# Cross-attention row stacks: permuted weight columns for longer reads, one write of the score rows, six filling matmuls before each first half

## The reference, cut to what matters

```
x = layernorm(x + causal_attention(x))            # one head, width 256
Q, K, V = x Wq' + bq, ctx Wk' + bk, ctx Wv' + bv  # 16 heads of 16
per head, blocks of 128 queries and keys:
  local = softmax(Q_b K_b' / 4) V_b
  cross = softmax(Q_b K_w' / 4) V_w               # w: blocks b-1, b, b+1 inside the sequence
x = layernorm(x + (local + cross) Wo' + bo)
x = layernorm(x + top2_of_8_experts(x) + shared_expert(x))
```

## Time and profile before

| | |
|---|---|
| median of 3 runs | 935.84 us (932.71 to 937.98) |
| profiled execution, its own time | 933.65 us |
| its span, first to last instruction | 931.9 us |
| mean granted TensorE clock | 0.907 of full |
| PE busy, share of the span | 89% |
| DVE, ACT, POOL busy | 43%, 37%, 26% |
| DMA traffic | 76.83 MB, mean 82 GB/s |

### The profile page before, as it was taken

One profiled execution on the slowest core, in us unless ns is written; L12 is line 12 of the kernel. 1 busy time (PEld: TensorE's weight loads), 2 busy tenths in 40 slices (PEclk: granted clock), 3 DMA queues, 4 the chain that ended last, 5 costly groups with the idle time before them and its releaser, 6 DMA issues. The chain is left out here.

```text
span 931.9 us, 15553 instructions
## 1 busy us (share of the span) xinstructions
PE 830.1 (89%) x4992; PEld 626.3 (67%) x4993; DVE 397.5 (43%) x746; ACT 346.7 (37%) x898; POOL 242.0 (26%) x258
## 2 busy tenths in 40 slices
PE   6689988999898989999579998999999999999930
PEld 4567765777567656766479997666777777666620
DVE  4736574568346844452376552211222222222216
ACT  1122454346343633255254430333333333333313
POOL 6912111123111401020416775211111111111106
PEclk9987995799669975999889999999999999999975
DMA  9962133121404080300191115541111101111035
GB/s 305 159 178 51 47 94 91 44 52 50 135 2 91 19 231 3 70 4 2 49 363 42 57 52 131 182 158 34 34 34 34 33 29 34 34 34 32 19 108 179
DMA packets 61045, 76.83 MB, mean 82 GB/s; under 512 B 16112, under 2 KB 41584, under 8 KB 60880
## 3 DMA queue, kind: packets, MB, share of 16 engines
q1 hardware_dynamic: 57600, 66.99, 25.9%
q0 software_dynamic: 3408, 9.34, 2.8%
HBM read 50.82 MB, written 24.98 MB: 81 GB/s over the span
## 5 line engine op out<-in xcount | busy, mean ns | idle before, releaser
L1023 DVE TENSOR_REDUCE mx<-ps 128x4 f32<-128x512 f32 (+1 forms) x128 | 104.4, 821 | 95.4 <-PE ps L1507 93.9
L1694 PE MATMUL ps<-we,hT 128*128 x624 | 142.8, 382 | 2.5 <-ACT hT L795 2.5
L1694 PEld LDWEIGHTS ps<-we,hT 128*128 128x128 f32 x624 | 119.7, 192 | 35.5 <-issue 20.9
L1674 PE MATMUL ps<-we,xT 128*128 x312 | 140.6, 593 | 1.9 <-issue 1.9
L1224 DVE COPY hp<-ps 128x512 f32<-128x512 f32 x78 | 50.2, 686 | 158.5 <-PE ps L1674 158.5
L1507 PE MATMUL ps<-k_stack,q_stack 96*128 96x256 f32 (+1 forms) x256 | 88.9, 441 | 16.2 <-DMA q_stack<-q_rows 14.2
L795 ACT ACTIVATE hT<-ps,b1T 128x128 f32<-128x128 f32 x312 | 84.9, 383 | 35.2 <-PE ps L1685 35.2
L1674 PEld LDWEIGHTS ps<-we,xT 128*128 128x128 f32 x312 | 56.2, 190 | 58.1 <-issue 58.1
L697 ACT ACTIVATE pT<-ps 128x256 f32<-128x256 f32 x128 | 49.2, 385 | 117.9 <-PE ps L1522 113.1
L1507 PEld LDWEIGHTS ps<-k_stack,q_stack 96*128 96x128 f32 x256 | 50.6, 246 | 54.5 <-issue 24.4
L590 ACT ACTIVATE xT<-ps 128x256 f32<-128x256 f32 x39 | 14.9, 384 | 180.9 <-PE ps L1657 180.9
(11 more groups left out here) (214 smaller groups left out, 1246.1 us busy)
## 6 DMA issues: line engine op xcount, KB each, us to landing
we<-in_w SPq DMA_DIRECT2D x16, 1024.0 KB, 10.6
k_stack<-k_rows SPq DMA_DIRECT2D x24, 256.0 KB, 4.0
q_stack<-q_rows SPq DMA_DIRECT2D x96, 64.0 KB, 4.1
slot_rows<-attn SPq DMA_DIRECT2D x1, 4992.0 KB, 25.0
xs<-slot_rows SPq DMA_DIRECT2D x39, 128.0 KB, 2.1
k_rows<-k_s SPq DMA_DIRECT2D x16, 256.0 KB, 2.3
q_rows<-q_s SPq DMA_DIRECT2D x16, 256.0 KB, 2.8
yl<-pair_out SPq DMA_DIRECT2D x4, 1024.0 KB, 9.5
```

The source lines that it names most:

```text
L1023: nc.vector.tensor_reduce(mx[:, n, 2 * p:2 * p + 2, r0:r0 + nb], ps[:, 2 * (u % 2):2 * (u % 2) + 2, 0:nb * P].rearrange("p h (b k) -> p h ...
L1674: m = nc.tensor.matmul(ps[:, 2 + c, :], xT[:, q, k, :], w[:, bass.ds(e, 1), k * HID + c * 512:k * HID + (c + 1) * 512].rearrange("p o n -> ...
L1694: m = nc.tensor.matmul(ps[:, 6, 0:D], hT[:, c, :], w[:, bass.ds(e, 1), KD * HID + c * D:KD * HID + (c + 1) * D].rearrange("p o n -> p (o n)"),
```

## The change

1. The columns of the cross-attention's `Wq` and `Wk` and their biases are permuted (on the host, where the weights are laid out), the same way for both, so that the 16 or 32 rows of a pair are interleaved: row `4 r + g` is row `r` of pair `g`. A `k_stack` read then takes, for each partition, 4 adjacent rows (8 KB), a `q_stack` read 2 adjacent rows (4 KB). Heads of `q_stack` change their place (`at` below), and so do the heads in `aug`.
2. High and low parts have semaphores of their own, and the order of the `q_stack` reads is by part first.
3. The four aug rows go in one DMA.
4. At the end of each `project2` with a `c` (three of them) PE waits for the combination (`cb_out`) and runs six `keep_clock` matmuls into bank 0.

```diff
+WARM_Q = 6
...
-                    sp.dma_start(rows[h, part], src[:, h, part, :].bitcast(F)).then_inc(away[h], 16)
+                    sp.dma_start(rows[h, part], src[:, h, part, :].bitcast(F)).then_inc(away[2 * h + part], 16)
...
-                sp.wait_ge(k_away[h], 32 * b + 32)
-                for sec, part in ((0, 0), (2, 0), (1, 1)):
-                    sp.dma_start(k_stack[32 * sec:32 * sec + 32, h * PAIRS:(h + 1) * PAIRS, :].bitcast(F),
-                                 k_rows[h, part].rearrange("(g p) t -> p g t", g=PAIRS)).then_inc(stacked[h], 16)
-                sp.wait_ge(q_away[h], 32 * b + 32)
+            def stack_keys(b, h):
+                for part, secs in ((0, (0, 2)), (1, (1,))):
+                    sp.wait_ge(k_away[2 * h + part], 16 * b + 16)
+                    for sec in secs:
+                        sp.dma_start(k_stack[32 * sec:32 * sec + 32, h * PAIRS:(h + 1) * PAIRS, :].bitcast(F),
+                                     k_rows[h, part].rearrange("(r g) t -> r g t", g=PAIRS)).then_inc(stacked[h], 16)
+            def stack_queries(b, h):
                 for part_done, g0 in ((stacked, 0), (stacked_late, PAIRS // 2)):
-                    for par in range(2):
-                        for sec, part in enumerate((0, 0, 1)):
-                            r = 32 * sec + 16 * par
-                            at = h * HALF + 2 * g0 + par
-                            sp.dma_start(q_stack[r:r + 16, at:at + HALF // 2 - 1:2, :].bitcast(F),
-                                         q_rows[h, part].rearrange("(g a p) t -> a p g t", g=PAIRS, a=2)
-                                         [par][:, g0:g0 + PAIRS // 2, :]).then_inc(part_done[h], 16)
+                    for part, secs in ((0, (0, 1)), (1, (2,))):
+                        sp.wait_ge(q_away[2 * h + part], 16 * b + 16)
+                        for sec in secs:
+                            for par in range(2):
+                                r, at = 32 * sec + 16 * par, h * HALF + PAIRS * par + g0
+                                sp.dma_start(q_stack[r:r + 16, at:at + PAIRS // 2, :].bitcast(F),
+                                             q_rows[h, part].rearrange("(a r g) t -> a r g t", a=2, g=PAIRS)
+                                             [par][:, g0:g0 + PAIRS // 2, :]).then_inc(part_done[h], 16)
...
-                for r in range(4):
-                    sp.dma_start(q_stack[96 + r:97 + r, h * HALF:(h + 1) * HALF, :].bitcast(F),
-                                 augT[r * HALF:(r + 1) * HALF, :].bitcast(F)).then_inc(s["aug_in"], 16)
+                sp.dma_start(q_stack[96:100, h * HALF:(h + 1) * HALF, :].bitcast(F),
+                             augT[:, :].bitcast(F)).then_inc(s["aug_in"], 16)
...
-                    nc.vector.tensor_copy(aug[:, :, 0, :], ncross[:, :, :]).then_inc(s["aug_step"], 1)
+                    nc.vector.tensor_copy(by_pair(aug[:, :, 0, :]), ncross4).then_inc(s["aug_step"], 1)
...
-                if c is None:
-                    keep_clock(WARM, bank=0)
+                if c is not None:
+                    pe.wait_ge(s["cb_out"], c + 1)
+                keep_clock(WARM if c is None else WARM_Q, bank=0)
                 pe.wait_ge(s["qk2_lo"], 4 * b + 4)
...
-                                                 q_stack[0:96, ha * HALF + 2 * p + j, n * P:(n + 1) * P],
+                                                 q_stack[0:96, ha * HALF + PAIRS * j + p, n * P:(n + 1) * P],
...
-                        qv = q_stack[:, 2 * p:2 * p + 2, :]
+                        at = hc * HALF + p % PAIRS
+                        qv = q_stack[:, at:at + PAIRS + 1:PAIRS, :]
...
+    order = np.arange(D).reshape(2, PAIRS, 2, DH).transpose(0, 2, 3, 1).reshape(D)
+    for n in ("L0_xattn_Wq", "L0_xattn_Wk"):
+        lay[n] = lay[n][:, order]
```

More of the change, by code:

```diff
@@ L222, in build @@
                                             for n in ("xs_in", "yw_sent", "st_step", "st_sent"))
-        k_away, q_away, stacked, stacked_late = ([sem(f"s_{n}{h}") for h in range(2)]
-                                                 for n in ("k_away", "q_away", "stacked", "stacked_late"))
+        k_away, q_away = ([sem(f"s_{n}_away{h}_{part}") for h in range(2) for part in ("hi", "lo")] for n in "kq")
+        stacked, stacked_late = ([sem(f"s_{n}{h}") for h in range(2)] for n in ("stacked", "stacked_late"))
         yl_in = [sem(f"s_yl_in{b}") for b in range(B)]
@@ L298, in body @@
                     sp.wait_ge(s["b_ps"], 2 * UNITS * (2 * b - 1))
-                stack(b, 0)
-                keys_away(b, 1)
-                queries_away(b, 1)
+                stack_keys(b, 0)
+                stack_queries(b, 0)
+                rows_away(b, 1, k_rows, k_s, k_away, 1)
+                rows_away(b, 1, q_rows, q_s, q_away, 2)
                 if not last:
@@ L314, in body @@
                     sp.wait_ge(s["b_ps"], 2 * UNITS * (2 * b))
-                stack(b, 1)
+                stack_keys(b, 1)
+                stack_queries(b, 1)
                 if not last:
@@ L319, in body @@
                         .then_inc(s["c_raw_in"], 16)
-                    keys_away(b + 1, 0)
+                    rows_away(b + 1, 0, k_rows, k_s, k_away, 1)
                 aug_rows(b, 1)
                 if not last:
-                    queries_away(b + 1, 0)
-            keys_away(0, 0)
-            queries_away(0, 0)
+                    rows_away(b + 1, 0, q_rows, q_s, q_away, 2)
+            rows_away(0, 0, k_rows, k_s, k_away, 1)
+            rows_away(0, 0, q_rows, q_s, q_away, 2)
             body(0, True, False)
@@ L596, in aug_rows @@
                 if free:
-                    act.wait_ge(s["aug_in"], 64 * a)
+                    act.wait_ge(s["aug_in"], 16 * a)
                 act.wait_ge(s["augT_ps"], a + 1)
@@ L665, in project2 @@
                 if c is not None:
-                    for h in range(2):
-                        act.wait_ge(k_away[h], 32 * b)
-                        act.wait_ge(q_away[h], 32 * b)
+                    for away in k_away + q_away:
+                        act.wait_ge(away, 16 * b)
                 projected(0)
@@ L1030, in half @@
                     at = 3 * a
+                    by_pair = lambda x: x.rearrange("p n (a g) -> p n g a", a=2)
+                    ncross4 = ncross[:, :, :].rearrange("p n (g a) -> p n g a", a=2)
+                    dloc4 = dloc[:, h, :, :].rearrange("p n (g a) -> p n g a", a=2)
                     dve.wait_ge(s["a_red"], UNITS * a + UNITS)
@@ L1034, in half @@
                     nc.vector.tensor_tensor(dloc[:, h, :, :], mx[:, :, :, 1], ncross[:, :, :], ALU.subtract)
-                    nc.vector.tensor_copy(aug[:, :, 0, :], ncross[:, :, :]).then_inc(s["aug_step"], 1)
+                    nc.vector.tensor_copy(by_pair(aug[:, :, 0, :]), ncross4).then_inc(s["aug_step"], 1)
                     dve.wait_ge(s["aug_step"], at + 2)
-                    nc.vector.tensor_tensor(aug[:, :, 1, :], ncross[:, :, :], aug[:, :, 0, :].bitcast(F), ALU.subtract)
-                    nc.vector.tensor_copy(aug[:, :, 2, :], dloc[:, h, :, :]).then_inc(s["aug_step"], 1)
+                    nc.vector.tensor_tensor(by_pair(aug[:, :, 1, :]), ncross4, by_pair(aug[:, :, 0, :]).bitcast(F), ALU.subtract)
+                    nc.vector.tensor_copy(by_pair(aug[:, :, 2, :]), dloc4).then_inc(s["aug_step"], 1)
                     dve.wait_ge(s["aug_step"], at + 3)
-                    nc.vector.tensor_tensor(aug[:, :, 3, :], dloc[:, h, :, :], aug[:, :, 2, :].bitcast(F), ALU.subtract)\
+                    nc.vector.tensor_tensor(by_pair(aug[:, :, 3, :]), dloc4, by_pair(aug[:, :, 2, :]).bitcast(F), ALU.subtract)\
                         .then_inc(s["aug_ready"], 1)
@@ L1494, in half @@
                     pe.wait_ge(s["k_ones"], 1)
-                    pe.wait_ge(s["aug_in"], 64 * (c + 1))
+                    pe.wait_ge(s["aug_in"], 16 * (c + 1))
                 for u in range(UNITS):
@@ L1755 @@
         lay[n] = a[n].T if "xattn" in n or n == "L0_attn_Wv" else a[n]
+    order = np.arange(D).reshape(2, PAIRS, 2, DH).transpose(0, 2, 3, 1).reshape(D)
+    for n in ("L0_xattn_Wq", "L0_xattn_Wk"):
+        lay[n] = lay[n][:, order]
+    a["L0_xattn_bq"], a["L0_xattn_bk"] = a["L0_xattn_bq"][order], a["L0_xattn_bk"][order]
     lay["brow"] = np.stack([a["L0_attn_bo"], a["L0_xattn_bv"], a["L0_xattn_bo"]])
```

5 lines of the change are left out of this document (removed).

## The result

The changed kernel takes 918.54 us, the median of five executions (908.97, 909.47, 918.54, 929.92, 930.79), against 935.91 us for the kernel before (five, 932.71 to 937.98). The ratio is 0.9742 [0.9691, 0.9792]; it leaves the two executions at 930 us out as possibly disturbed, and with all five the ratio of the medians is 918.54 / 935.91 = 0.981. It is faster, by 17.4 us at the medians of all five (24 us by the ratio), where I had forecast 44, and outside my range of 884 to 908 us.

The account below looks back on a forecast made before the run. PE's stalls for query reads before three first halves, and the halved clock they set off, were taken as the bound. Clock 37 us plus earlier starts 7.1 us made 44: 935.84 - 44 gives about 892 us, range 884 to 908.

Parts of the forecast that it names:

- What bounds the kernel, and what the clock costs: First halves of bodies 1 to 3: stalls cost some 13 us, the 1.2 GHz clock they set off 3 x 12.3 = 37 us.
- One aug write: SP's queue before the first halves: three calls fewer start body 1 1.1 us earlier, bodies 2 and 3 2.0 us each.
- rival 3: The four-row aug write clogs its DMA engines; PE starts 3.1 us later three times, clock lost, 945 us; chance 0.04.
- Longer runs: Stack reads in longer runs land faster; between no gain and the 397 GB/s of `x_raw`, the middle was taken.
- the lower bound: Longer runs bring no gain: stack reads land as far apart as before, 1.1 to 1.5 us for 256 KB.
- Rival 1: Stack reads come no faster: start gain 5.1 us, 893.7 us, or 906 if body 1's clock is lost (0.11).
- the start gain: Earlier starts of the three first halves together: 5.1 us without faster reads, 9.1 with the full rate, 7.1 taken.
- The clock: All three first halves keep full clock, as idle times lie below stalls of 1.92 us (kept) and 2.48 us (lost): 37 us.
- the middle case: Stack reads gain half the possible rate: start gain 7.1 us, idle about 1 us or less before each first half.
- all three hold: Case where the three first halves keep full clock, whatever the reads' rate: 890 to 894 us, chance 0.72.
- two are lost, about 918: Case where two of the three first halves lose full clock: about 918 us, chance 0.05.
- Slower: Outcome for the whole kernel: changed kernel slower than before by more than 0.5% (4.7 us), chance 0.05.

## Why the prediction was wrong

**What bounds the kernel, and what the clock costs.** Right in kind. The three stalls and the three halves at 1.2 GHz were where the time was, and when they were gone 37.4 us were gone. The size of the clock's price was a little off: 34.5 us, not 3 x 12.3 = 37. "At full clock ACT and DVE keep up in a first half" failed for body 3, where PE waits 2.8 us for DVE's `aug`. I had compared with a second half, which has other work behind it.

**One aug write.** The call's price was right (0.65 to 0.67 us where four took 2.71). For body 1 I counted 1.1 us, and the start moved 1.8; with four writes and the rest of the change it comes 1.1 us later, so the count was right for the write, and 0.7 us came from parts that I had put at nothing or from scatter. The sentence that failed is "In bodies 2 and 3 PE gets to the queries earlier against SP's queue, and I take the whole 2.0 us". SP did reach the `k_stack` reads 2.6 and 2.1 us sooner, but the starts moved by 1.1 and 0.6 us: behind the single write the query writes landed a microsecond and more later, and SP waited for them. A mild form of rival 3 had come true. I had priced it from 0.18 us a run at 1.4 us on four engines and called it harmless, because I looked only at whether the write's own end would pass 133.2, and not at what it would do to the writes just behind it. The DMA share while it runs is about 0.25 (after, stretches of half a us in body 1):

```profile
131.50:132.00 0.50, 0.50 (x7) 0.50 (x6) 0.32 (x1) 0.27 (x2) 0.00 (x0) 1.00 0.26 66
132.00:132.50 0.50, 0.50 (x8) 0.50 (x5) 0.43 (x1) 0.00 (x0) 0.00 (x0) 1.00 0.23 70
```

0.25 of 16 engines is four of them. By the Trainium skill (DMA: Bandwidth & Descriptors, on why a DMA increments its semaphore by 16) the slowest dimensions of source and destination decide the number, here four, and this agrees. It agrees for the kernel with two writes as well, where it gives two engines, 0.125 of 16; in body 1 of that kernel:

```profile
131.75:132.25 0.50, 0.50 (x8) 0.50 (x6) 0.48 (x1) 0.00 (x0) 0.00 (x0) 1.00 0.11 41
```

The number of engines does not tell how long the queries behind are held: with two writes it was shorter in bodies 2 and 3.

**Longer runs.** "I take the middle" was wrong; the lower bound was right. Rival 1 (the reads come no faster) came true, but for the tenth of a microsecond. I had the rule that says so, and a measured spacing near it, and still took half of the upper bound from `x_raw`. With the lower bound and the whole 2.0 us the start gain would have been 5.1 us; it was 3.5.

**Six fillers.** They took 1.55 us (1.4 forecast) and hid in idle time, and the wait for the combination cost nothing. The fillers' starts against the key writes are as forecast.

**The clock.** This is the step in which the prediction fell: "the idle times that I expect (about 1 us or less in the middle case) lie below both". They were 1.41, 2.03 and 2.26 us. The middle case counted starts 2.15, 2.6 and 2.4 us earlier; they came 1.8, 1.1 and 0.6 us earlier, and the missing 0.4, 1.5 and 1.8 us are the excess of the stalls over the forecast. The term of the sum that was mis-sized is the start gain, 3.5 us in place of 7.1; what it did, by way of the stalls, was to cost two of the three clocks, some 21 us of the 37. And the two marks of the earlier trace rows, 1.92 us kept and 2.48 us lost, come from the expert part; before a first half, 1.27 us was enough once. I had named the zone between 1.92 and 2.48 us as open and given "all three hold" 0.72 all the same. The profiled execution is the case "two are lost, about 918", to which I gave 0.05. My chances treated the three halves as nearly one event that goes well; they are three, each near the edge, and differ from one execution to the next: the five took 909 us twice, 918.5 and 930 twice. Only the one at 918.5 was profiled (two lost). The two at 909 us have clocks of 0.936 and 0.938, as if one had been lost; the two at 930 us show 0.908 and 0.910, close to the 0.907 of the kernel before, as if all three had been; both are inferred and not shown.

**Slower (0.05).** No execution was. The sign was right.

**What the best version is.** The changed kernel with sixteen fillers, about 898 us; its six executions lie within 2.5 us, while twelve have the same median and lost about 10 us in two of six. The permutation can be left out (897.2 us).

## What to carry to other kernels

When a stall drops the TensorE clock, the stall is the small part of its price: here 13 us of stalls set off 34.5 us. Fill such a gap to the landing of what PE waits for and a little beyond: sixteen fillers start body 1's half 0.9 us later than twelve, while the one to two microseconds that six and nine left uncovered cost 9 to 12 us a time, in some executions and not in others.

Before crediting an earlier issue as an earlier start, follow the queue to the next thing that must land. And where the trace gives a spacing and a rule explains it, take it, and not the mean with a bound from a transfer of another shape.

## What the runs showed of the hardware that I had not expected

- The clock can fall after the work has started again: in body 2 it stood at 1.00 through the stall and the first 1.5 us of the half, in body 3 through the stall and the first 0.6 us, then fell while PE was busy all the time. In body 3, and, in the last line, in body 3 of the kernel before, where the half began at 337.53 at full clock behind a stall of 4.26 us:

```profile
322.50:323.00 0.50, 0.50 (x4) 0.18 (x2) 0.50 (x2) 0.50 (x2) 0.00 (x0) 0.84 1.04 393
323.00:323.50 0.50, 0.50 (x2) 0.50 (x3) 0.50 (x2) 0.16 (x1) 0.00 (x0) 0.50 1.10 422
...
338.00:338.50 0.50, 0.50 (x5) 0.41 (x3) 0.46 (x1) 0.33 (x2) 0.00 (x0) 0.58 0.96 270
```

- Once down it stayed at 1.2 GHz for the rest of the half, 28.5 us of PE without a gap. In body 2 it was back at 1.00 in the stretch from 258 to 259 us, in the projection that follows the half (from 256.98).
- The times of one kernel lie on steps, 909, 918.5 and 930 us for the changed one. Whether the stalls differed between these executions, or the clock's answer to the same stall, is not shown, as only one of them was profiled.
- One 64 KB write into four partitions delays what is issued just behind it: in body 3 two writes of 256 KB landed after 3.5 us instead of 2.2, and after 2.0 once it was moved behind them; in body 2 they still took 3.3 us. Four writes of 16 KB ahead did no such harm (2.0 to 2.7 us).
